# A two-layer vision transformer on one core: the six transfers that fill each query tile issued half from SP's queue and half from ACT's

## What is computed

```python
q = (jnp.einsum('bte,oe->bto', x, Wq) + bq) * scaling          # 256 = 16 heads x 16
kv = jnp.einsum('bte,oe->bto', x, Wkv) + bkv
k, v = (kv[..., :HEAD_DIM], kv[..., HEAD_DIM:])                 # one head each
qr = q.reshape(bsz, NUM_HEADS * tgt_len, HEAD_DIM)
attn_weights = jnp.einsum('brd,bsd->brs', qr, k)
attn_probs = jax.nn.softmax(attn_weights, axis=-1)
attn_output = jnp.einsum('brs,bsd->brd', attn_probs, v)
...
out = jnp.einsum('bte,oe->bto', attn_output, Wo) + bo
```

## Time and profile before

| | us |
|---|---|
| median of 3 runs | 1063.58 |
| lowest and highest run | 1062.18, 1065.08 |
| span of the profiled execution | 1059.6 |
| the attention phase in it, about | 144 to 425 |
| TensorE busy in the span | 745.2 (70%) |
| ACT busy in the span | 243.6 (23%) |

### The profile page before, as it was taken

One profiled execution on the slowest core, in us unless ns is written; L12 is line 12 of the kernel. 1 busy time (PEld: TensorE's weight loads), 2 busy tenths in 40 slices (PEclk: granted clock), 3 DMA queues, 4 the chain that ended last, 5 costly groups with the idle time before them and its releaser, 6 DMA issues. The chain is left out here.

```text
span 1059.6 us, 17440 instructions
## 1 busy us (share of the span) xinstructions
PE 745.2 (70%) x5222; PEld 591.4 (56%) x5223; DVE 428.3 (40%) x1314; ACT 243.6 (23%) x671; POOL 247.5 (23%) x379
## 2 busy tenths in 40 slices
PE   6999547758557668269999820039910599999995
PEld 5877436646446557158888620028810276676673
DVE  2444313333333334636666630946630133333331
ACT  0000012222222222144433310005410123222221
POOL 2111012222222222003333410014337022222321
PEclk9999855575775675569999955559955699999998
DMA  4444200100000000056000014910056211211110
GB/s 157 134 133 135 57 9 9 11 9 9 9 9 9 9 9 4 1 124 136 0 0 0 0 11 110 407 33 13 9 186 134 55 51 45 50 54 45 50 45 20
DMA packets 80034, 60.67 MB, mean 57 GB/s; under 512 B 58044, under 2 KB 72006, under 8 KB 79494
## 3 DMA queue, kind: packets, MB, share of 16 engines
q1 hardware_dynamic: 63674, 40.95, 15.4%
q0 software_dynamic: 10368, 11.76, 4.5%
q10 hardware_dynamic: 5964, 7.60, 2.2%
HBM read 41.19 MB, written 19.07 MB: 57 GB/s over the span
## 5 line engine op out<-in xcount | busy, mean ns | idle before, releaser
L536 PE MATMUL bank<-cst,arena_w 111*96 111x111 f32 x176 | 37.7, 395 | 101.3 <-DMA arena_w<-q_rows 80.3
L248 POOL TENSOR_TENSOR work<-work 111x1 f32<-111x1 f32 x88 | 48.5, 551 | 235.4 <-DVE work L244 235.4
L1779 PE MATMUL bank<-arena_w,work 128*128 x208 | 97.1, 611 | 1.0 <-DVE work L1831 1.0
L1803 PE MATMUL bank<-arena_w,work 128*128 x416 | 94.2, 380 | 0.4 <-ACT work L1878 0.4
L1878 ACT ACTIVATE work<-bank,cst 128x128 f32<-128x128 f32 x208 | 56.4, 382 | 144.9 <-PE bank L1792 144.9
L536 PEld LDWEIGHTS bank<-cst,arena_w 111*96 111x96 f32 x176 | 29.7, 196 | 106.1 <-DMA arena_w<-q_rows 85.0
L1803 PEld LDWEIGHTS bank<-arena_w,work 128*128 128x128 f32 x416 | 77.2, 191 | 10.3 <-issue 1.1
L1441 PE MATMUL bank<-tokens,work 111*111 (+1 forms) x88 | 16.1, 310 | 87.1 <-POOL work L1410 86.2
L814 POOL TENSOR_TENSOR work<-work 111x592 f32<-111x592 f32 x22 | 26.3, 1195 | 202.2 <-DVE work L665 202.2
L662 DVE TENSOR_REDUCE work<-work 111x16 f32<-111x592 f32 x22 | 16.9, 770 | 139.5 <-ACT work L736 139.5
L316 PE MATMUL bank<-arena_w 128*111 128x256 f32 x264 | 65.0, 399 | 8.8 <-DMA arena_w<-in_pack 8.8
(11 more groups left out here) (208 smaller groups left out, 1482.8 us busy)
## 6 DMA issues: line engine op xcount, KB each, us to landing
arena_w<-in_w SPq DMA_DIRECT2D x2, 4096.0 KB, 13.5
arena_w<-in_x SPq DMA_DIRECT2D x22, 333.0 KB, 3.2
x_slots<-arena_w SPq DMA_DIRECT2D x1, 6682.0 KB
tokens<-x_slots SPq DMA_DIRECT2D x26, 128.0 KB, 2.1
tokens<-x_slots POOLq DMA_DIRECT2D x26, 128.0 KB, 2.3
arena_w<-in_pack ACTq DMA_DIRECT2D x11, 256.5 KB, 4.7
q_rows<-work ACTq DMA_DIRECT2D x22, 111.0 KB
arena_w<-q_rows SPq DMA_DIRECT2D x132, 18.5 KB
```

The costliest lines, as they stand in the source:

```text
L248: nc.gpsimd.tensor_tensor(ve[j][:, 1:2], ve[j][:, 0:1], ve[j][:, 2:3], ALU.pow).then_inc(s_rs[j], 1)
L536: mm = nc.tensor.transpose(bank[2 + half][0:KR, k * R:(k + 1) * R], qx[j][:, a:a + KR], ident[0:R, 0:R])
L1779: mm = nc.tensor.matmul(bank[2 * j + f][:, :], xgt[j][:, k * 128:(k + 1) * 128], arena_w1[:, bass.ds(expert * (2 * FF) + (k * FF + f * 512 ...
L1803: mm = nc.tensor.matmul(bank[7][:, 0:D], ht[j][:, g * 128:(g + 1) * 128], arena_w2[:, bass.ds(expert * (FC * D) + g * D, D)], start=(g == ...
```

## The change

`load_queries` takes the engine and the parities it is to issue. In the second phase SP issues the three transfers of the even heads and ACT the three of the odd heads. ACT issues them for tile n+3 right behind its copies of the turned queries of tile n+1 (the same buffer), and ahead of L744. ACT's turns start one pair earlier, so that the loads of tile 2 are issued behind the copies of tile 0. Tiles 0 and 1 are loaded as before. Line numbers behind this place grow by 13.

```diff
--- before.py
+++ after.py
@@ -250,13 +250,13 @@
         def norm_apply(out, x, j):
             return nc.vector.tensor_scalar(out, x, st[j][:, 6:7], ve[j][:, 1:2], ALU.subtract, ALU.mult)
 
-        def load_queries(sp, i, j):
+        def load_queries(eng, i, j, parities):
 
 
             for m in range(IPT):
                 src = q_rows[bass.ds((2 * i + j) * R + m * TOK, TOK), :].rearrange("t (g d) -> (t g) d", d=HD)
-                for e in range(2):
-                    sp.dma_start(
+                for e in parities:
+                    eng.dma_start(
                         qx[j][m * TOK:(m + 1) * TOK, :].rearrange("t (c m e d) -> t c m e d", m=IPT, e=2, d=HD)[:, :, m, e, :],
                         src.rearrange("(c e t) d -> t c e d", e=2, t=TOK)[:, :, e, :]).then_inc(q_in[j], 16)
 
@@ -294,7 +294,7 @@
                 sp.wait_ge(zero_ready, 6)
                 for j in range(2):
                     sp.wait_ge(q_stored[j], 16)
-                    load_queries(sp, 0, j)
+                    load_queries(sp, 0, j, range(2))
 
             @block.tensor
             def _(pe):
@@ -512,7 +512,7 @@
                     for j in range(2):
                         wait_free(sp, q_turned[j], i)
                         sp.wait_ge(q_stored[j], 16 * i + 16)
-                        load_queries(sp, i, j)
+                        load_queries(sp, i, j, range(1))
 
                 turn(1)
                 with sp.Fori(2, PAIRS) as i:
@@ -760,22 +760,35 @@
                     nc.scalar.copy(x_t.rearrange("p (k n) -> p k n", k=2)[:, :, bass.ds((2 * i + j) * R, R)],
                                    xt[j].rearrange("p (k n) -> p k n", k=2)).then_inc(x_saved[j], 1)
 
+                def load_odd_heads(pair_at, j):
+                    if pair_at is None:
+                        return
+                    i, n1 = pair_at
+                    if isinstance(i, int) and i == 0:
+                        return
+                    act.wait_ge(q_turned[j], i)
+                    act.wait_ge(q_stored[j], 16 * n1)
+                    load_queries(act, i, j, range(1, 2))
+
                 def turn(i):
                     last, this, following = at(act, i, -1), at(act, i), at(act, i, 1)
+                    after = at(act, i, 2)
                     copy_probs(last, 1)
                     copy_queries(this, 1)
+                    load_odd_heads(following, 1)
                     copy_output(last, 1)
                     exponentials(this, 0)
                     copy_rows(last, 0)
                     save_rows(last, 0)
                     copy_probs(this, 0)
                     copy_queries(following, 0)
+                    load_odd_heads(after, 0)
                     copy_output(this, 0)
                     exponentials(this, 1)
                     copy_rows(last, 1)
                     save_rows(last, 1)
 
-                run_turns(act, turn, ahead=1, behind=1)
+                run_turns(act, turn, ahead=2, behind=1)
 
             @block.gpsimd
             def _(pool):
```

## The result

The changed kernel takes 1145.88 us in the median of 3 runs (1145.15 to 1148.21), against 1063.58 before: a ratio of 1.078, 95% interval 1.074 to 1.082. The profiled span is 1146.6 us, 87.0 more.

The account below looks back on a forecast made before the run. The attention stage was taken as bound by 64 B packets, 12.94 us per tile; afterwards by ACT's hold plus lap, 18.61 or 15.47 us, giving +108 or +46, weighted +92: median 1063.6 to 1156 us, range 1095 to 1190.

Parts of the forecast that it names:

- The bound before: Attention stage: a tile's 1776 packets of 64 B, one per 7.34 ns without pause, set its period of about 13.0 us.
- Two queues don't add: SP's and ACT's queues share one server packet by packet; 7.34 ns per packet and 12.94 us per tile stay.
- The hold X: ACT's three issues per tile behind L728 hold its sequencer 8.26 us, from an empty queue, until earlier packets are served.
- The lap beside it, C: From ACT's release at L744 through TensorE's work to L728's end: 10.35 us at 1.2 GHz, 7.21 us with 2.4 GHz.
- high-clock lap: Lap beside ACT's hold with the clock up to 2.4 GHz: 4.50 us to L567's end plus 2.71, 7.21 us.
- The clock: TensorE in the attention stage gets 2.4 GHz a quarter of the time, turning +108 us into +92.
- The sum: 19 periods plus start and end: +108 us low clock, +46 high, +92 taken; span 1152 us, median 1156.
- the main range: Main case, chance 0.77: +46 to +125 us, 1110 to 1189; top is low clock plus 1 us per tile of unseen delays.
- ACT isn't held: Rival, chance 0.10: ACT's queue takes 888 packets without holding the sequencer; 0.87 us per tile goes into slack, 1064 us.
- Parallel: Rival, chance 0.06: two queues served in parallel, 6.5 us of packets per tile; 1037 us all high clock, 1100 all low.
- Locked: Rival, chance 0.07: ACT also waits for SP's issues, hold 11.7 us, 18.9 to 22.05 us per tile, 1225 us.

Follow-up runs that it names:

- the late version: The changed kernel with ACT's three issues moved behind the saving of the rows (L760): 1052.48 us, ratio 0.990 to the kernel before.

## Why the prediction was right, step by step

*The bound before.* Right, and sharper than it was put: a tile's transfers set the pace because each is served at the rate of one DMA engine. The Trainium skill has the rule ("DMA: Bandwidth & Descriptors", section "Why a DMA increments its semaphore by 16 and not by 1"): a transfer from SP or ACT is spread over the largest number of engines up to 16 that divides the slowest dimension of both its sides. The runs agree: 37 rows and 31 rows leave TensorE waiting 75 and 85 us, 36 rows 12.5 us. The packet counts agree too: beside its runs of 64 B a transfer of 37 rows has one packet of 4 bytes (891 for three), one of 36 rows has twelve (300 for 288 runs), and 1 and 12 are what the rule gives. Which engine served a packet, the traces don't show. One reading was off: the packets of the kernel before do pause, 10.4 us in 19 laps.

*Two queues don't add.* Right in the main: 1079 packets of both queues in 8.65 us after the start at 419.2 are 8.0 ns each with the start-up, and the late version ran at 7.05 ns through all laps. Two queues are 4% faster than one (7.34 ns), which I had at nothing, since either fills the other's pauses. 33744 packets in 19 laps make that up to 10 us; the late version's laps gained 5.5.

*The hold X.* Forecast 8.26 us; 8.74 in the lap shown. The shape was forecast as 0.3, 3 and 4 us, and the issues of 419 us on took 0.25, 3.58 and 4.52. The forecast let SP's queue have as many packets served as ACT's 497; from 419.2 on it was 594 beside 485. In four laps, whose issues stand outside ACT's loop, the hold was shorter, 6.87 to 7.04 us; there ACT issued first (171.90) and SP second (172.10). What of that shortens it, no run isolates:

```profile
171.90 3.25 ACTq L259 DMA_DIRECT2D arena_w<-q_rows  x2
...
175.18 3.59 ACTq L259 DMA_DIRECT2D arena_w<-q_rows  x1
178.81 0.34 ACT L744 COPY arena_w<-bank 128x222 f32<-128x222 f32 x1 [6.00 <-issue]
```

At the start the queue was not empty, as X assumes: ACT's second hold lasted from 152.91 to 165.35, 12.4 us. The lap over it took 22.03 us, and 18.61 + 3.4 had been forecast for it; that the two agree is chance.

*The lap beside it, C.* Mis-sized: 10.35 us at the low clock was forecast, 9.26 measured. L744's start to L567's end is 246.84 to 254.48, 7.64 us, to the hundredth what the earlier trace rows gave. The rest, 2.71 us from L536's start to L728's end, was wrong twice: L536 follows L567 without a pause and overlaps it by 0.2, and the issue didn't wait for the copies ahead of it: it started at 256.01, where the second L728 began at 256.18. L744, behind the issues, waited for them in all 17 laps of the list above. The forecast's high-clock lap (7.21 us) has the same fault, with an L536 taken at the low clock: the last lap, with no hold, took 6.87 us at a clock of 0.79.

*The clock.* A quarter of the time at 2.4 GHz was forecast to shorten the laps. The stage had 0.57, a seventh of the time, but in none of the 14 middle laps were L549 and L567 shorter than at the low clock. The high clock came into the waits, as these windows (clock third from the end) show; TensorE was busy 0.55 of 3.30 us in the first:

```profile
238.30:241.60 3.30, 0.55 (x25) 0.29 (x14) 0.00 (x0) 0.42 (x1) 0.00 (x0) 1.00 0.07 7
241.70:255.20 13.50, 7.96 (x38) 7.50 (x39) 4.36 (x12) 2.62 (x6) 2.96 (x5) 0.50 0.07 7
```

*The sum, and how much of it was luck.* For the 19 laps +96 us had been forecast (107.7 + 3.4, less 15 for the clock), and +94.1 came. At the low clock throughout the forecast's terms give 17 us more than was measured: 14 laps took 18.13 us rather than 18.61 (the hold 0.5 us longer, the rest 1.1 shorter), 7 us in all, and the four with the short hold 64.1 rather than 74.4 us, 10 more. The discount for a high clock that didn't come to the work, 15 us, stood in for them. The mechanism was right; that the laps agree to 2 us is luck. The last lap gave 6.2 back rather than about 3.5. So the span grew by 87.0 and not 92, and 4.7 of the 10 us between 1156 and 1145.88 are no term of the kernel: the forecast put the median 4.0 us above the profiled span, and it lies 0.7 below it. (The top of the main range has a slip: 108 + 19 is 127, not 125.)

*The rivals.* "ACT isn't held" is refuted by ACT's own records. "Parallel" is refuted by the 7.05 ns that two queues need per packet. "Locked" had a hold of 11.7 us where 8.74 came, and in the version with one of six on ACT its issue at 265.93 took 0.25 us inside one of SP's that ran from 265.17 to 267.23. Of the exclusive lock that the Trainium skill states ("Perfetto Trace Analysis", section "DMA Instruction — HWDGE (DVE, Sync)") that issue shows no cost.

## What to carry to other kernels

Before moving a transfer to a compute engine's queue, look at how long its issue lasts where it is: here 2 us rather than 0.25 meant that it waited for earlier packets, and on ACT all that followed waited with it. If it must go there, put it where that engine would idle, not between an input that has arrived and the work on it. And if small transfers are the bound, look at the number of rows first: cutting 37 rows into 36 and 1 was worth 10% (31 and 6 lost 1.5%), the best choice of queue and place 1%.

## What was not expected of the hardware

- An issue ended when about 100 packets of the transfers before it were left (97, 109, 95), beside its own 149 or 297.
- One queue paused 104 times between packets, 10.4 us in 19 laps; with two queues there was no pause, 7.05 ns per packet against 7.34.
- 36 partitions rather than 37 took a load from being the bound (12.94 us per tile) to below 8.4 us.
- Halving the transfers that ACT issues made the hold longer, from 8.7 to 11.9 us.
